# An audio block with two expert stages: the next tile's transposes ahead of the up product on TensorE

## The reference, cut to what matters

```python
# stage one: every row goes to its 2 best of 8 experts
router_probs = jax.nn.softmax(x @ w_gate)
top_p, top_i = jax.lax.top_k(router_probs, 2)
h = jax.nn.gelu(x @ w_fc[expert], approximate=True)      # 192 -> 768
o = h @ w_proj[expert]                                   # 768 -> 192
out = sum over the two experts of o * top_p
...
# stage two: every sequence of 32 rows goes to its best of 3 experts
h = jax.nn.gelu(x @ W1[expert] + b1[expert], approximate=False)
y = h @ W2[expert] + b2[expert]
out = y * score
```

## Time and profile before

| | us |
|---|---|
| median of 3 runs | 558.98 (557.87 to 562.82) |
| the profiled execution | 562.9 |
| its span, first to last instruction | 561.0 |
| TensorE matmul busy | 500.1 (89%) |
| VectorE busy | 360.8 (64%) |
| ScalarE busy | 260.7 (46%) |
| GpSimd busy | 225.8 (40%) |
| stage one, first up product to last | 209.40 to 384.48 |
| stage two, first up product to last | 467.41 to 545.60 |

### The profile page before, as it was taken

How to read it: one execution, slowest core, us unless ns; L and a number is a source line. 1 busy time by engine, 2 the same in 40 slices (tenths; PEclk the granted TensorE clock), 3 DMA queues, 4 the chain that set the end, 5 groups by cost and what they waited for, 6 DMA issues and landing times.

```text
span 561.0 us, 15458 instructions
## 1 busy us (share of the span) xinstructions
PE 500.1 (89%) x5695; PEld 449.3 (80%) x5695; DVE 360.8 (64%) x999; ACT 260.7 (46%) x771; POOL 225.8 (40%) x316
## 2 busy tenths in 40 slices
PE   8999999999897058999999999999999997999993
PEld 7677768888786058889898889898888886998993
DVE  2576579989999584555555555554357665666661
ACT  2678868695566232222222222222457642453541
POOL 1255540016786333444444444432212214444422
PEclk9999989999999669999999999999999998999998
DMA  9992000008001101131221311210733323122110
GB/s 259 244 200 42 3 0 2 0 2 336 16 30 37 35 24 36 48 84 43 80 51 44 87 44 44 43 38 31 232 112 100 92 73 84 51 67 72 58 37 21
DMA packets 32379, 40.73 MB, mean 73 GB/s; under 512 B 7121, under 2 KB 27730, under 8 KB 32306
## 3 DMA queue, kind: packets, MB, share of 16 engines
q1 hardware_dynamic: 25586, 25.39, 16.7%
q0 software_dynamic: 5760, 12.98, 8.1%
q10 hardware_dynamic: 960, 1.38, 0.9%
HBM read 29.41 MB, written 10.32 MB: 71 GB/s over the span
## 4 chain that ended last, share of the span: by engine, by line
PE 48%; issue 5%; ACT 4%; another core or an unknown queue 4%; DVE 3%; POOLq 0%; DVEq 0%; POOL 0%; ACTq 0%
PE psum L1565 20%; PE psum L1577 14%; PE psum L1547 4%; PE psum L1956 3%; PE psum L1960 2%; PE psum L137 1%; PE psum L1967 1%; ACT hidden_room L1602 1%; ACT rows_turned L1915 1%; ACT rows_turned L1592 1%; PE psum L1713 1%; DVE hidden_room L1315 1%; PE psum L1948 1%; ACT hidden_room L1604 0%
## 5 line engine op out<-in xcount | busy, mean ns | idle before, releaser
L1565 PE MATMUL psum<-rows_turned,expert_weights 64*128 64x128 f32 x2052 | 130.6, 278 | 13.2 <-ACT rows_turned L1592 9.2
L1565 PEld LDWEIGHTS psum<-rows_turned,expert_weights 64*128 64x128 f32 x2052 | 122.8, 190 | 24.5 <-issue 24.2
L1577 PE MATMUL psum<-expert_second_weights,hidden_room 64*128 64x192 f32 x1368 | 125.4, 327 | 2.2 <-issue 2.2
L1577 PEld LDWEIGHTS psum<-expert_second_weights,hidden_room 64*128 64x128 f32 x1368 | 112.1, 187 | 2.7 <-issue 2.7
L1590 ACT ACTIVATE rows_turned<-psum 128x192 f32<-128x192 f32 x57 | 18.9, 331 | 181.5 <-PE psum L1547 151.7
L1529 POOL DMA_INDIRECT y<-rows_out,out_row_by_slot x39 | 45.7, 1171 | 90.2 <-DVE rows_out L1659 90.2
L1657 DVE COPY rows_out<-psum 128x192 f32<-128x192 f32 x39 | 14.0, 358 | 74.5 <-PE psum L1577 74.5
L1522 POOL DMA_INDIRECT rows_in<-x,token x39 | 42.9, 1099 | 22.4 <-issue 11.6
L855 PE MATMUL psum<-arena 97*128 97x512 f32 (+1 forms) x192 | 49.5, 417 | 0.5 <-ACT h L600 0.5
L855 PEld LDWEIGHTS psum<-arena 97*128 97x128 f32 (+1 forms) x192 | 37.8, 200 | 9.9 <-ACT h L600 0.9
L919 DVE SCALAR_TENSOR_TENSOR conv_out<-psum,param,conv_out 128x496 f32<-128x496 f32 (+2 forms) x60 | 41.9, 715 | 3.2 <-ACT conv_out L867 1.8
(11 more groups left out here) (284 smaller groups left out, 974.3 us busy)
## 6 DMA issues: line engine op xcount, KB each, us to landing
w_proj<-in_w_proj SPq DMA_DIRECT2D x8, 576.0 KB, 7.6
sz<-in_x SPq DMA_DIRECT2D x16, 192.0 KB, 7.9
w_fc<-in_w_fc SPq DMA_DIRECT2D x4, 768.0 KB, 18.7
w<-in_w SPq DMA_DIRECT2D x3, 576.0 KB, 4.1
w_fc<-in_w_fc SPq DMA_DIRECT2D x4, 384.0 KB, 17.0
x<-xf_tile SPq DMA_DIRECT2D x16, 96.0 KB, 1.6
expert_rows<-y SPq DMA_DIRECT2D x8, 192.0 KB, 4.1
hidden_room<-y SPq DMA_DIRECT2D x8, 192.0 KB, 4.6
```

The costliest lines, as they stand in the source:

```text
L1565: done = nc.tensor.matmul(ps_h[t.odd][half][:, ch, :], w_now[at, t.odd, first:first + P], xt[at, t.odd, block, :], start=block == 0 and ch ...
L1577: done = nc.tensor.matmul(ps_y[half], hid[at, t.odd, ch, :], w_down_now[at, t.odd, ch * D:(ch + 1) * D], start=ch == 0, stop=ch == HC - 1)
```

## The change

In the list that orders TensorE's queue, the transposes of the next tile come first in a step, before the up product; nothing else differs. The queue runs transposes of i+1, up(i), down(i-1), transposes of i+2, up(i+1), and so on. The list is used by both stages.

```diff
-        pipelined(pe, n_tiles, [(2, up), (1, turn_rows), (3, down)], 4, straight=True)
+        pipelined(pe, n_tiles, [(1, turn_rows), (2, up), (3, down)], 4, straight=True)
```

## The result

The changed kernel takes 539.2 us in the median of 4 runs (537.51 to 544.12), the kernel before 559.75 (557.87 to 562.82, 4 runs). The ratio is 0.9642, with a 95% interval of 0.9565 to 0.9719. The profiled execution took 537.51 us, with a span of 535.7 and a mean granted clock of 0.973. Some executions, in either order, showed a granted clock of 0.955 or less and took longer.

A forecast was written before the change was run, and what follows sets the result against it. TensorE's up product was held by ScalarE's late copies of turned rows. Terms 15.0 + 0.7 + 0.9 + 6.4 + 1.2 = 24.2, taken as 23.5 off the profiled 562.9, scaled to 535.5 us; range 532 to 545.

The forecast's parts named there:

- rival one: Steady tiles: the GpSimd and VectorE loop sets the pace at up to 4.37 us; about 541 us, chance 0.17.
- The steady tiles: Both stages' tiles fall to TensorE's own 4.193 us; 15.0 plus 0.67 us in stage one, 6.4 in stage two.
- 1.63 of low clock: Stage two's start: one up product at granted clock 0.50 after TensorE idled, counted as regained but not certain.
- The starts: Each stage's start: up(0) later, up(1) earlier; gains of 0.9 us in stage one and 1.2 in stage two.
- The mechanism: Steady tiles: increments TensorE posts while GpSimd issues indirect DMAs become visible only after them, making ScalarE 1.32 us late.
- 4.17 us after down's end: Steady tile: when up's held increments appear, from scatter start 1.18, gather 1.49 after it and 1.50 more.
- The slack of 2 us: Steady tile: turned rows ready at about 1.4 us (2.2 in stage two), wanted by the next up product at 4.2.
- Rival two: Nothing regained: the transposes' late increment is their true end, a tile is 4.68 us of work; 559 us, chance 0.08.
- the loop of the forecast: Down's end to scatter, gather and release of held increments: 4.17 us, or 4.37 in stage two, against a 4.19 tile.
- The slack absorbed the rest: Down's wait for its rows taken has about 1.5 us of slack, spent after eight tiles, then 0.18 us a tile.
- Rival three: Transposes ahead of up block TensorE if VectorE falls over 2.8 us behind; 5.55 us a tile, 602 us, chance 0.03.

The follow-up runs named there:

- stage_two_alone: The kernel before with the new queue order in stage two only, the old one in stage one; 557.84 us in one run on chip B.
- Experiment 4: Old order in stage one, gathers then scatters moved off GpSimd, then additions there; stage two's transposes two tiles ahead; 555.34 us against 555.84 before.
- experiment 5: Changed kernel plus a GpSimd addition between scatter and gather from stage one's tile 12, and four filler products before stage two's second transposes; 548.95 us against 555.84.
- new_order_again: The changed kernel repeated on chip E against the kernel before; 540.42 us, ratio 1.0072.
- stage_one_alone: The kernel before with the new queue order in stage one only, the old one in stage two; 540.15 us on chip A, ratio 1.0018.
- old_order_in_thirds: Kernel of Experiment 4: stage one in old order with three states of GpSimd work, stage two's transposes two tiles ahead; 555.34 us against 555.84.

## Why the prediction was right

**The time.** 535.5 was forecast and 539.2 measured, just above the 532 to 539 given to the forecast itself and inside the whole range of 532 to 545. By the time alone rival one's 541 lies nearer; the profile decides between them, by the 4.200 us a tile. Part of the 3.7 us is in how the forecast went from the profiled execution to the median: the profiled one fell from 562.9 to 537.51, 25.4 us (23.5 were forecast), and the medians by 20.5. The profiled execution of before was the slowest of its three, that of after the fastest of its four, so a share of the one could not be laid on the median to better than about 1%. The two stages became 23.8 us shorter, where the sum had 24.2.

**The steady tiles.** Forecast 15.0 + 0.67 = 15.67 for stage one without its start. From the first down product on, stage one became 16.48 - 0.94 = 15.5 shorter. The tile went from 4.678 to 4.200, not to 4.193: 0.007 x 31 = 0.2 us. In stage two, 6.4 with 1.63 of low clock in it makes 4.8, and measured was 7.32 - 2.82 = 4.5.

**The starts.** From the first transposes to the first down product stage one's start became 0.94 us shorter (7.61 to 6.67), with 0.9 forecast; stage two's 2.82 (9.79 to 6.97), with 1.2 + 1.63 = 2.83 forecast. up(0) was to be 0.9 us later and came 2.32 after the first transposes, where it was 1.19: 1.13 later. Tile 1's transposes took 0.32 us before the filler behind them began, not 0.18, as the timeline of TensorE at stage one's start has it:

```profile
207.88 0.40 PE L1547 MATMUL psum<-const,rows_twice 64*128 64x64 f32 x6 [0.73 <-ACT rows_turned L1592]
208.20 0.94 PE L137 MATMUL psum<-const 128*128 128x128 f32 x6
209.07 2.28 PE L1565 MATMUL psum<-rows_turned,expert_weights 64*128 64x128 f32 x36
```

The 1.63 us of low clock were regained here, but the idle they were put down to is not all there is to it: stage_two_alone has the new order and TensorE idle for 1.68 and 1.01 us ahead of its two first transposes, as the changed kernel has (1.71 and 1.01), and yet its up(0) took 4.12 us at a granted clock of 0.50. It depends on the run, so this term came true in part by luck.

**The mechanism.** That GpSimd's indirect DMAs hold what TensorE posts was an inference from the place of the lateness. Experiment 4 shows it for the chip it ran on: with the gathers gone the copy is 0.38 us late and the tile 4.193, with additions 0.00. In the changed kernel the lateness went where the forecast put it, to up's increments, but the size was off: they were to appear 4.17 us after down's end, and appear at 231.56 - 228.13 = 3.43 in the tile shown, within the gather and not 1.50 us after its start, and earlier in most others. The transposes' own increments weren't free either: the copy comes 0.03 us after them in the tile shown, but 0.1 to 0.34 in about half of the tiles of stage one, as at 245.49 after an end at 245.25, with the last gather over at 244.97. The slack of 2 us covers that. When exactly a held increment is let go stays open; these two places and down's increment in experiment 5 don't fit a release at the gather's end.

**Rival two** is refuted: the 4.68 us are not work of TensorE, since the old order runs at 4.193 on chip A with its gathers in place, and on chip D, which holds, without them. By the rule of the Trainium skill (Perfetto Trace Analysis, section Tensor Engine Instruction) the late increment could have been the true end of the transposes; with additions beside it, on a chip that holds, the same six transposes release ScalarE at their recorded end.

**Rival one** exists, at a small price. Stage two after, in the timeline: GpSimd's scatters, the down products, and VectorE's taking of rows.

```profile
467.23 1.15 POOL L1529 DMA_INDIRECT out<-rows_out,out_row  x1 [1.84 <-DVE rows_out L1664]
467.79 2.19 PE L1577 MATMUL psum<-expert_second_weights,hidden_room 64*128 64x192 f32 x24
...
470.47 0.42 DVE L1662 SCALAR_TENSOR_TENSOR w_fc<-psum,score_by_slot,w_fc 128x192 f32<-128x192 f32 x1 [1.21 <-PE psum L1577]
471.62 1.00 POOL L1529 DMA_INDIRECT out<-rows_out,out_row  x1 [1.84 <-DVE rows_out L1664]
471.99 2.19 PE L1577 MATMUL psum<-expert_second_weights,hidden_room 64*128 64x192 f32 x24
...
474.79 0.42 DVE L1662 SCALAR_TENSOR_TENSOR w_fc<-psum,score_by_slot,w_fc 128x192 f32<-128x192 f32 x1 [0.62 <-PE psum L1577]
```

The scatters are 4.39 us apart here, the down products 4.20: the loop of the forecast (4.37), which TensorE outruns. It doesn't stay there: the scatters of 497.31, 501.57 and 505.83 are 4.26 apart. Down's rows were to be taken 0.15 us after its end; here it is 470.47 - 469.98 = 0.49 and 474.79 - 474.18 = 0.61, and it grows to about 1.0. Then TensorE waits: the three tiles from 499.34 took 4.247 us each, 3 x 0.05 = 0.16 us in all, before the stage ends. The slack absorbed the rest over some ten tiles, where the forecast had eight. In stage one the loop stays below TensorE's pace; rows are taken 0.14 to 0.55 us late there.

**Rival three** didn't come: VectorE was never behind by the 2.8 us it would have taken.

**What the prediction missed** is not a term of its sum. It took the lateness for a property of the program on this hardware, and it is one of the chip. On the chips A, C and E the program before takes 538 us, no increment of TensorE is late in the steady tiles of their traces, and the change is worth nothing. By the traces it costs about 0.4 us there: stage one lasts 167.05 us in new_order_again against 166.98 in the old order without indirect DMAs (chips A and C), stage two 79.41 against 79.12 in the old order of stage_one_alone. The averages on chip E are 1.4 us apart, and single executions of the kernel before lie between 536.5 and 542 at a clock of 0.96 and more, so a larger cost isn't shown. The kernel before was not profiled on these chips; the old order was, in a stage of stage_one_alone. The time came out right because it was measured where the profile had been taken, on a chip that holds. Why some chips hold increments is open, and the changed kernel itself was timed on no second chip that does.

## What to carry to other kernels

An engine that starts late although what it waits for is over by the record is worth 0.5 us a tile here, and the cure is to look at what else runs beside it (here GpSimd's indirect DMAs) and to move the wait with the least slack out of that stretch, not to make anything faster. Where transposes move ahead of a product, put the filler ahead of them as well, into the wait that they bring (0.9 us a stage). Before believing a gain that rests on such lateness, time both kernels on a second and a third chip: this one was 3.6% on one and nothing on another.

## What the runs showed of the hardware

- One program took 561.45 us on chip F and 537.99 on chip E, 4.4% apart. In the old order's steady tiles of stage one, with a scatter and a gather beside the transposes, ScalarE takes them 1.29 to 1.54 us late on F, B and the chip of the first comparison, and 1.43 us late in the tile shown of D. On A, C and E it takes the steady tiles' transposes within 0.04 us of their end.
- On chip D the transposes' increment was held by indirect DMAs alone: with a scatter beside it, it appeared 0.23 us after the scatter's end, and three additions of 256 columns held nothing. Down's increment inside a gather appeared 0.17 us after down's end (experiment 5).
- What VectorE posts inside an indirect DMA was not late on chip D: in ten tiles of stage two of old_order_in_thirds its repeated rows are ready within a scatter (496.23 in 496.06 to 497.22), and TensorE's transposes start 0.05 to 0.06 us later.
